# A GRU step on one core: three of the four blocks of R from h, Y with h stationary, the R seed ahead of Z

## The reference

```python
def step(H, xs):
    xz, xr, xh = xs            # X @ W.T + b, for all steps
    Z = sigmoid(xz + H @ Whz.T + bhz)
    R = sigmoid(xr + H @ Whr.T + bhr)
    H_tilda = tanh(xh + R * H @ Whh.T + bhh)
    H_new = Z * H + (1.0 - Z) * H_tilda
    Y = H_new @ Whq.T + bhq
    return (H_new, Y)
# result: x + Ys
```

## Time and profile before

| | |
|---|---|
| median of three runs | 581.74 us |
| the profiled execution | 582.49 us, of which the span is 580.4 us |
| PE busy | 556.9 us (96%), 49372 matmul records |
| PEld busy | 545.5 us (94%) |
| DVE busy | 322.7 us (56%) |
| ACT busy | 289.6 us (50%) |
| DMA | 16.2% of 16 engines on the queue of x and the output |
| granted clock of PE | full, but for one stretch near the start |

### The profile page before, as it was taken

The page is one execution under the profiler, slowest core; times in us unless marked ns, Lnnn a source line. Parts: engine busy times, 40 slices in busy tenths (PEclk is TensorE's granted clock), DMA queues, the critical chain, the costliest instruction groups (busy, mean ns, idle before and its releaser), DMA issues.

```text
span 580.4 us, 105994 instructions
## 1 busy us (share of the span) xinstructions
PE 556.9 (96%) x49372; PEld 545.5 (94%) x49372; DVE 322.7 (56%) x1802; ACT 289.6 (50%) x1671; POOL 0.2 (0%) x4
## 2 busy tenths in 40 slices
PE   7599999999999999999999999999999999999996
PEld 6589999999999999999999999999999999999996
DVE  1145555555555655555655555555555555555554
ACT  2145555545545555555455554554555555555553
POOL 0000000000000000000000000000000000000000
PEclk9599999999999999999999999999999999999999
DMA  4011111111111111111111111111111111111111
GB/s 154 17 35 48 41 50 45 41 52 43 45 50 41 49 46 42 52 42 45 50 41 49 45 41 50 45 45 50 41 46 49 41 50 45 45 50 41 47 48 46
DMA packets 57880, 27.58 MB, mean 48 GB/s; under 512 B 7056, under 2 KB 56976, under 8 KB 57872
## 3 DMA queue, kind: packets, MB, share of 16 engines
q1 hardware_dynamic: 56736, 26.63, 16.2%
q10 hardware_dynamic: 1136, 0.83, 0.4%
HBM read 18.91 MB, written 8.52 MB: 47 GB/s over the span
## 4 chain that ended last, share of the span: by engine, by line
PE 96%; issue 3%; DMA 0%; DVE 0%; ACT 0%; SPq 0%; DVEq 0%; ACTq 0%
PE r_ps L232 38%; PE c_ps L232 25%; PE z_ps L232 22%; PE y_ps L232 11%; DMA xres_sb<-in_xt_dram 0%; DVE o_sb L199 0%; SPq L122 0%; ACT c_ps L147 0%; DVE u_sb L218 0%; ACT r_ps L147 0%; ACT c_sb L174 0%; ACT z_ps L147 0%; DVEq L30 0%; DVE ones_sb L185 0%; DVE h_sb L223 0%
## 5 line engine op out<-in xcount | busy, mean ns | idle before, releaser
L232 PE MATMUL c_ps<-xt_sb,wx_sb 128*32 128x64 f32 x4128 | 174.6, 226 | 1.5 <-issue 1.5
L167 ACT ACTIVATE r_sb<-r_ps 128x32 f32<-128x32 f32 x512 | 74.3, 197 | 152.4 <-PE r_ps L232 152.4
L213 DVE TENSOR_TENSOR rh_sb<-r_sb,h_sb 128x32 f32<-128x32 f32 x512 | 75.1, 188 | 101.0 <-ACT r_sb L167 101.0
L232 PE MATMUL r_ps<-u_sb,whr_sb 128*32 128x32 f32 x8192 | 122.0, 198 | 8.9 <-issue 2.6
L232 PE MATMUL r_ps<-zh_sb,whr_sb 128*32 128x32 f32 x8192 | 124.9, 197 | 3.5 <-issue 3.5
L232 PE MATMUL z_ps<-h_sb,whz_sb 128*32 128x32 f32 x8192 | 124.5, 198 | 0.0
L218 DVE SCALAR_TENSOR_TENSOR u_sb<-z_sb,c_sb 128x32 f32<-128x32 f32 x512 | 75.2, 188 | 83.7 <-ACT c_sb L174 83.7
L232 PE MATMUL c_ps<-rh_sb,whh_sb 128*32 128x32 f32 x8192 | 121.7, 198 | 0.0
L232 PEld LDWEIGHTS r_ps<-u_sb,whr_sb 128*32 128x32 f32 x8192 | 103.4, 112 | 19.0 <-issue 19.0
L232 PE MATMUL y_ps<-h_sb,whq_sb 128*32 128x64 f32 x4128 | 118.2, 224 | 0.3 <-DVE o_sb L199 0.3
L232 PE MATMUL z_ps<-xt_sb,wx_sb 128*32 128x64 f32 x4128 | 113.7, 220 | 2.7 <-issue 2.7
(11 more groups left out here) (26 smaller groups left out, 257.5 us busy)
## 6 DMA issues: line engine op xcount, KB each, us to landing
xt_sb<-in_xt_dram SPq DMA_DIRECT2D x130, 64.0 KB, 1.8
xres_sb<-in_xt_dram SPq DMA_DIRECT2D x130, 64.0 KB, 1.8
out_dram<-o_sb SPq DMA_DIRECT2D x130, 64.0 KB, 1.6
wx_sb<-in_wx_dram SPq DMA_DIRECT2D x2, 256.0 KB, 4.3
wx_sb<-in_wx_dram ACTq DMA_DIRECT2D x1, 256.0 KB, 4.9
whz_sb<-in_whz_dram SPq DMA_DIRECT2D x1, 256.0 KB, 5.3
whr_sb<-in_whr_dram ACTq DMA_DIRECT2D x1, 256.0 KB, 6.0
whq_sb<-in_whq_dram SPq DMA_DIRECT2D x1, 256.0 KB, 6.3
```

Of the source, the lines that this page charges most:

```text
L167: nc.scalar.activation(r_sb[:, o], r_ps[:, o, here], ACT.Sigmoid).then_inc(s_r[o], 1)
L213: nc.vector.tensor_tensor(rh_sb[:, k], r_sb[:, k], old[:, k], ALU.mult).then_inc(s_rh[k], 1)
L232: return nc.tensor.matmul(ps, weights, moving, start=start, stop=False, skip_group_check=True, **kw)
```

## The change

R: of the four blocks of the product, one (k = 1, o = 0) stays split into a zh part, ahead of time, and a u part. The three others are taken from h itself, which was not needed there before. For this, h is added in two halves with a semaphore each (`s_h[k]`), and `rh_sb` waits for its half of h. The prologue does one block in place of four.

Y: a 32-column tile of h of one step is the stationary operand and 128 rows of `whq_sb` are moving, so Y comes out with the batch on the partitions. The four column tiles hold the two steps of a chunk and the two output halves, so one block does one half k of the contraction for all of the chunk: one block of four matmuls with 128 columns in a step, in place of two blocks with 64. The bias of Y, now a 128x128 tile, is written into PSUM by ACT once a chunk (`seed_y`), behind the sigmoid of Z in the second step; the first one ahead of the loop waits for the load of `bq_sb`. DVE adds the residual once a chunk, in its first step, in one instruction over 128 columns, with the residual's x and the output laid out to match.

Order: on ACT the R seed stands ahead of the sigmoid of Z. On PE the second x block of Z stands behind the candidate's blocks.

```diff
+            def seed_y(p):
+                return nc.scalar.copy(y_ps[p][:, 0, 0:P], bq_sb[:])
...
+            act.wait_ge(s_bq, DMA)
+            seed_y(1).then_inc(s_seed_y, CS)
...
+                    if s == 0:
+                        seed(r_ps[:, :, W * (1 - p):W * (1 - p) + W], R).then_inc(s_seed_r, CS)
                     act.wait_ge(s_z_ps, t + 1)
                     nc.scalar.activation(z_sb[:], z_view(p)[:, :, B * s:B * s + B], ACT.Sigmoid).then_inc(s_z, 1)
-                    if s == 0:
-                        seed(r_ps[:, :, W * (1 - p):W * (1 - p) + W], R).then_inc(s_seed_r, CS)
+                    if s == CS - 1:
+                        act.wait_ge(s_res, t + CS)
+                        seed_y(p).then_inc(s_seed_y, CS)
...
+            def residual(p, chunk, row_dmas):
+                dve.wait_ge(s_rows[p], row_dmas)
+                dve.wait_ge(s_y_ps, chunk + PAD + 1)
+                nc.vector.tensor_tensor(o_sb[:, p], y_ps[p][:, 0, 0:P], xres_sb[:, p], ALU.add).then_inc(s_res, CS)
...
-                    dve.wait_ge(s_h, t + 1)
                     for k in range(K):
+                        dve.wait_ge(s_h[k], t + 1)
                         dve.wait_ge(s_r[k], t + 1)
...
                     for k in range(K):
                         dve.wait_ge(s_u[k], t + 2)
-                    nc.vector.tensor_tensor(new, zh_sb[:], u_sb[:], ALU.add).then_inc(s_h, 1)
-                    residual(p, s, i * 2 + p - PAD, i * (2 * DMA) + DMA)
+                        nc.vector.tensor_tensor(new[:, k], zh_sb[:, k], u_sb[:, k], ALU.add).then_inc(s_h[k], 1)
+                    if s == 0:
+                        residual(p, i * 2 + p - PAD, i * (2 * DMA) + DMA)
...
-                return columns(y_ps[p][:, 0], slice(W * o, W * o + W), whq_sb, k, o,
-                               h_sb[:, k, CS * p:CS * p + CS], start=piece == 0)
+                for j in range(NQ):
+                    half, step = divmod(j, CS)
+                    last = mm(y_ps[p][B * j:B * j + B, 0, 0:P], h_sb[:, k, CS * p + step], whq_sb[:, k, P * half:P * half + P],
+                              tile_position=(0, B * j))
...
-                    for k in range(K):
-                        pe.wait_ge(s_u[k], t + 1)
-                        for o in range(K):
-                            r_mm = r_part(u, k, o, u_sb[:, k])
-                            if k == K - 1:
-                                r_mm.then_inc(s_r_ps[o], 1)
+                    pe.wait_ge(s_u[1], t + 1)
+                    r_part(u, 1, 0, u_sb[:, 1])
+                    pe.wait_ge(s_h[0], t + 1)
+                    r_part(u, 0, 0, old[:, 0]).then_inc(s_r_ps[0], 1)
+                    r_part(u, 0, 1, old[:, 0])
+                    pe.wait_ge(s_h[1], t + 1)
+                    r_part(u, 1, 1, old[:, 1]).then_inc(s_r_ps[1], 1)
...
-                    for piece in pieces:
-                        x_piece(q, Z, piece)
+                    x_piece(q, Z, pieces[0])
...
+                    x_piece(q, Z, pieces[1])
                     if s == 0:
                         pe.wait_ge(s_seed_r, t + 1)
...
                     pe.wait_ge(s_zh, t + 1)
-                    for k in range(K):
-                        for o in range(K):
-                            r_part((u + 1) % SLOTS, k, o, zh_sb[:, k])
-                    if s == 0:
-                        pe.wait_ge(s_res, t + 1)
-                    for piece in pieces:
-                        y_mm = y_piece(q, piece)
+                    for k, o in AHEAD:
+                        r_part((u + 1) % SLOTS, k, o, zh_sb[:, k])
+                    if s == 0:
+                        pe.wait_ge(s_seed_y, t + 1)
+                    y_mm = y_piece(q, s)
```

More of the change, by code:

```diff
@@ L20, with gru_kernel @@
 WARM = 60
-def gru_kernel(nc, xt, h0t, wx, whz, whr, whh, whq, bx, bh, bq, out):
+AHEAD = ((1, 0),)
+def gru_kernel(nc, xt, xr, h0t, wx, whz, whr, whh, whq, bx, bh, bq, out):
     fp32 = mybir.dt.float32
@@ L47, in gru_kernel @@
         b_sb = sb("b_sb", [P, K, 3])
-        bq_sb = sb("bq_sb", [P, K])
+        bq_sb = sb("bq_sb", [P, P])
         ones_sb = sb("ones_sb", [P, P], bf16)
         act_warm = sb("act_warm", [1, 1])
-        bq_seen = sb("bq_seen", [1, 1])
+        res_seen = sb("res_seen", [1, 1])
         xt_sb = sb("xt_sb", [P, 2, K, W])
-        xres_sb = sb("xres_sb", [P, 2, K, W])
-        o_sb = sb("o_sb", [P, 2, K, W])
+        xres_sb = sb("xres_sb", [P, 2, P])
+        o_sb = sb("o_sb", [P, 2, P])
         h_sb = sb("h_sb", [P, K, SLOTS, B])
@@ L97, in gru_kernel @@
         s_u = [sem(f"s_u{k}") for k in range(K)]
-        s_h = sem("s_h")
+        s_h = [sem(f"s_h{k}") for k in range(K)]
         s_zh = sem("s_zh")
@@ L190, in _ @@
                 nc.vector.memset(u_sb[:, k], 0.0).then_inc(s_u[k], 1)
[L191 to L202, removed]
+                nc.vector.memset(h_sb[:, k, CS], 0.0).then_inc(s_h[k], 1)
+            nc.vector.memset(res_seen[:], 0.0).then_inc(s_res, CS)
+            def residual(p, chunk, row_dmas):
+                dve.wait_ge(s_rows[p], row_dmas)
+                dve.wait_ge(s_y_ps, chunk + PAD + 1)
+                nc.vector.tensor_tensor(o_sb[:, p], y_ps[p][:, 0, 0:P], xres_sb[:, p], ALU.add).then_inc(s_res, CS)
             with dve.Fori(0, NIT) as i:
@@ L222, in _ @@
                         dve.wait_ge(s_u[k], t + 2)
[L223 to L224 removed]
+                        nc.vector.tensor_tensor(new[:, k], zh_sb[:, k], u_sb[:, k], ALU.add).then_inc(s_h[k], 1)
+                    if s == 0:
+                        residual(p, i * 2 + p - PAD, i * (2 * DMA) + DMA)
             for p in range(2):
[L226 to L227 removed]
+                residual(p, NC + p - PAD, NIT * (2 * DMA) + DMA)
         @block.tensor
@@ L247, in x_piece, with y_piece @@
                 return columns(ps, cols, wx_sb[:, gate], k, o, xt_sb[:, p, k])
-            def y_piece(p, piece):
-                o, k = divmod(piece, K)
-                return columns(y_ps[p][:, 0], slice(W * o, W * o + W), whq_sb, k, o,
-                               h_sb[:, k, CS * p:CS * p + CS], start=piece == 0)
+            def y_piece(p, k):
+                for j in range(NQ):
+                    half, step = divmod(j, CS)
+                    last = mm(y_ps[p][B * j:B * j + B, 0, 0:P], h_sb[:, k, CS * p + step], whq_sb[:, k, P * half:P * half + P],
+                              tile_position=(0, B * j))
+                return last
             def r_part(u, k, o, moving):
@@ L274, in _ @@
             pe.wait_ge(s_init, DMA)
-            for k in range(K):
-                for o in range(K):
-                    r_part(0, k, o, h_sb[:, k, SLOTS - 1])
+            for k, o in AHEAD:
+                r_part(0, k, o, h_sb[:, k, SLOTS - 1])
             pe.wait_ge(s_whz, DMA)
@@ L326, in _ @@
                     pe.wait_ge(s_zh, t + 1)
-                    for k in range(K):
-                        for o in range(K):
-                            r_part((u + 1) % SLOTS, k, o, zh_sb[:, k])
+                    for k, o in AHEAD:
+                        r_part((u + 1) % SLOTS, k, o, zh_sb[:, k])
                     if s == 0:
-                        pe.wait_ge(s_res, t + 1)
-                    for piece in pieces:
-                        y_mm = y_piece(q, piece)
+                        pe.wait_ge(s_seed_y, t + 1)
+                    y_mm = y_piece(q, s)
                     if s == CS - 1:
                         y_mm.then_inc(s_y_ps, 1)
[L337 to L340, removed]
+            pe.wait_ge(s_seed_y, T + 1)
+            for k in range(K):
+                pe.wait_ge(s_h[k], T + 1)
+            for k in range(K):
+                y_mm = y_piece(1, k)
             y_mm.then_inc(s_y_ps, 1)
@@ L361 @@
     chunks = x.transpose(2, 1, 0).reshape(K, P, NC, W).transpose(2, 1, 0, 3)
+    rows = x.reshape(B, NC, CS, K, P).transpose(1, 3, 2, 0, 4).reshape(NC, P, P)
     arrays = {
         "xt": np.pad(chunks, ((PAD, PAD), (0, 0), (0, 0), (0, 0))),
+        "xr": np.pad(rows, ((PAD, 0), (0, 0), (0, 0))),
         "h0t": np.asarray(cond_1024).T.reshape(K, P, B).transpose(1, 0, 2),
@@ L380 @@
                                    kind="ExternalInput").ap())
-    args.append(nc.dram_tensor("out_dram", (NC + PAD, P, K, W), mybir.dt.float32, kind="ExternalOutput").ap())
+    args.append(nc.dram_tensor("out_dram", (NC + PAD, P, P), mybir.dt.float32, kind="ExternalOutput").ap())
     gru_kernel(nc, *args)
@@ L384 @@
     rows = r.results[0]["out_dram"][PAD:]
-    return rows.reshape(NC, P, K, CS, B).transpose(4, 0, 3, 2, 1).reshape(B, T, C)
+    return rows.reshape(NC, K, CS, B, P).transpose(3, 0, 2, 1, 4).reshape(B, T, C)
```

9 lines of the change are left out of this document (4 added, 5 removed).

## The result

The changed kernel takes 557.83 us in the median of four runs (557.34 to 559.16); the kernel before takes 581.50. The ratio is 0.960, with a 95% interval of 0.957 to 0.963: 4% faster. The forecast was 562.0 us with 549 to 582 as its range.

A forecast was written before the change was run, and what follows sets the result against it. The prediction took PE as the old bound and the chain through h as the new one: 29.1 + 63 x 8.38 (528) + 3.1 = 560.2 us span, plus 2.1 around it, 562.3, given as 562.0 us; range 549 to 582.

The forecast's parts named there:

- the rival in which PE stays the bound: Rival: halves overlap better than the links say, so PE still bounds the step; 7.65 us a pass, 516 us; chance 0.05.
- The chain: Seven links from one step's first tanh through u, h, R's sigmoid, rh_sb and candidate to the next: 2.05 us.
- the path through the second halves: Same links by the second halves, each starting one to two blocks behind the first: same sum within 0.01 us.
- The disputed link, u to h: First half of h on DVE after u: 0.22 us taken; rival with second wait counting 0.29, 575.5 us, chance 0.20.
- the rival of the short group: Rival: sigmoid comes 0.46 us after R's first h block, not 0.33; step 2.18, 595 us; chance 0.07.
- The sign to look for: On PE, ahead of R from h: idle by some 0.2 us, released by DVE's h_sb.
- The loop turn: PE's 0.33 us at the end of a pass, beside the wait after Y, delays h's first block: 0.18 us a pass.
- The first pass: PE's code loading: five stalls instead of six, 3.8 us apart, so the second pass starts at 29.1 us.
- The end: After the last Y starts: 0.7 us for blocks and tail, 0.35 for DVE, 2.06 to the span's end; 3.1 us.
- Y: Y's one 128-column block on PE, in place of two with 64: 0.22 or, rounded, 0.23 us, against 0.24.
- The covers: Moved seeds and the wider residual cost nothing behind other work; the Y seed has 0.12 us to spare before the tanh.
- a failed cover: Rival: the cover of Y's seed or Z's sigmoid fails, taking back 0.07 to 0.1 us a step; 582 us; chance 0.06.

The follow-up runs named there:

- the experiment that forced the other case: Changed kernel with one more, always met, wait ahead of the first half of h, so u's wait stands in front: 582.87 us, ratio 1.002.

## Why the prediction was right, step by step

The bound changed hands as forecast: PE's records fell by some 128 a pass (769 to 642 in the windows), the clock stayed, and the chain by h set the step. That is shown from both sides: 0.07 off one link takes 18 us off the time, 0.09 more on another adds 25, and 0.22 more work on PE in each step costs 7. With a step of 2.08 against PE's 1.83, a pass of 8.32 and not 7.65, the rival in which PE stays the bound is out too. Against the terms of the sum:

- *The chain.* 2.05 predicted, 2.08 measured. Six of seven links are within 0.01 of their value; the seventh, candidate to tanh, was taken from the row of before as 0.47 and is 0.49, because R's two halves are now complete two blocks apart on PE: the second sigmoid, and with it the second half of `rh_sb`, comes 0.16 after the first instead of 0.10 (0.35 for both where the earlier trace rows has 0.29), and the candidate's second half waits for it on PE. The prediction had the sigmoids 0.13 apart (1.03 and 1.16), and held the path through the second halves to be the same within 0.01. The disputed link, u to h, is 0.23 against the 0.22 taken and 0.29 at the other end, and the experiment that forced the other case made it 0.32. The group of 8 records reached the sigmoid in 0.34 (0.33 taken), so the rival of the short group is out.
- *Where PE waits.* The sign to look for was some 0.2 ahead of R from h, released by `h_sb`. The larger wait, 0.15, lies ahead of R from u, and the table puts it down to `u_sb`; only 0.05 lie ahead of R from h. The sum of the chain does not change by that.
- *The loop turn.* 0.18 a pass predicted, 0.00 measured; this was the wrong term. I added its 0.33 to the end of Y (0.48 + 0.33 = 0.81). In the trace R from u starts 0.62 after the tanh at the turn and 0.58 elsewhere, ahead of h's 0.70. The turn is not a fixed length behind the last block: from Y's start to the next R it took 0.57 in the kernel before (0.24 of it work), 0.51 with Y in its old form, 0.53 with all of R split, 0.41 in the changed kernel. With as many records of Y, it is shorter where PE had waited more within the pass (16 records: 0.57 and 0.51; 8 records: 0.53 and 0.41). Why is open: that PE's sequencer runs ahead during such waits would fit, but no run tests it. With 0.03 more a step (0.12) and 0.18 less at the turn, a pass is 8.32 instead of 8.38: 3.8 us in 63 passes. That the pass came out so close is luck in part: the chain alone is 7.6 us too short in 63 passes, the turn 11.3 too long, and they cancel.
- *The first pass.* Five stalls in place of six, as said, 3.5 us apart (11.64 to 25.76), and the second pass starts at 26.9 instead of 29.1. One of these 2.2 us is there before the loop starts: it begins at 9.5 instead of 10.6, released by the load of `whh_sb`. That isn't the change's doing: the kernel before with only the seed moved also began at 9.5. The rest is hardly the clock's: that kernel had 1.00 through its first pass and took 22.0 us from the loop's start to the second pass; the kernel before, at 0.50 from 20 to 28 us, took 22.3; the changed one, at 0.75 from 20 to 24, took 17.4. The wait for `bq_sb` made ACT 0.3 us late once, under the first stall, as said.
- *The end.* 3.1 predicted, 3.9 measured, from the last Y (551.63) to 555.5. DVE's last instruction is released by PE, as said, but 1.20 after the block's start; 0.7 had been taken. Where the other 0.5 lies, no row shows. From DVE's end to the span's end there are 2.38 us where 2.06 had been taken.

```profile
551.63 0.65 PE L239 MATMUL y_ps<-whq_sb,h_sb 128*32 128x128 f32 x16 [0.27 <-DVE h_sb L230]
...
552.83 0.29 DVE L209 TENSOR_TENSOR o_sb<-y_ps,xres_sb 128x128 f32<-128x128 f32 x1 [0.97 <-PE y_ps L239]
```

- *Y.* 0.23 taken, 0.22 measured. The rule of the Trainium skill (TensorE: Matmul & The Clock Gate, Back-to-back issue gap), that starts are never closer than about 25 ns, does not hold for these matmuls, four side by side in column tiles: 24 records of R from h start within 0.22 us, 9 ns each.
- *The covers* held: Y's seed ran from 304.76 to 305.03 and the tanh started at 305.15 on its own time, 0.12 later as forecast. The residual over 128 columns takes 0.29 where I had 0.35. The clock stayed at 1.00 in steady passes, so the second failure mode of the clock that the Trainium skill tells of (same page, A second HAM failure mode) did not appear; the waits of this kernel are 0.05 to 0.15 us, and 0.19 at the loop turn.
- *Slips in the sums* that changed nothing here: 0.1 us a step of a failed cover would be some 588 us and not 584; the lower end of the range, 549, is 13 us below the forecast and not the 8 that the chain's 0.03 a step give; and the terms add up to 562.3, not 562.0.

What the forecast had not seen is how little R's part is worth here. The steps of the experiments add up: the seed 10 us (571.6), then Y in its new form with h in halves and the residual once a chunk, with all of R still split and Z's blocks in their old order, 8 us more (563.6), then R from h together with the moved block the last 6 (557.8). Of these 6, the pass has 0.04 x 63 = 2.5 (8.36 to 8.32), and the rest is the first pass with its one stall less (the second pass starts at 26.9 instead of 31.5). The kernel with only the second x block put back splits them another way: R from h by itself took 563.6 to 561.9, which is within noise, with a pass of 8.38 that is no shorter than 8.36; the moved block then took 4 us. PE was freed of 0.21 us a step, and the detour by h took back all of it. In the prediction it reads as if R's blocks carried the gain; the number came out right because the chain was summed up independently of them, and because the misses on chain and turn cancel in part.

## What to carry to other kernels

Where PE's order covers a chain exactly, price each edit twice: by what it takes off PE, and by the sum of the chain's links as they will be, and take the larger. That is what the forecast did right. A block moved past a wait counts as much as a block removed: an x block of 0.12 us moved behind the candidate cost 30 us, gained 4 us and cost 11 us in three neighbours of this kernel. Before moving any work, look at the order of the waits in front of the instructions on the chain: here the one that is met last has to be carried by the instruction, which gave 18 us for two swapped lines, and only 6 us where PE was the bound.

## What the runs showed of the hardware that I had not expected

- On DVE a releaser that a separate wait in front of the instruction waits for costs 0.07 us more than one that the instruction carries (sigmoid to `rh_sb` 0.30 against 0.23), and 0.09 to 0.10 where the front wait asks for two semaphores (0.32 against 0.23).
- The time that the turn of PE's loop adds depends on the work around it: 0.33 us in the kernel before, 0.19 at most in the changed one, and 0.08 where Y was issued twice.
- An addition of 128 columns out of PSUM takes 0.29 us, and the instruction before, with two additions over 64 columns, took 0.28. So twice the columns with one addition fewer cost 0.01; the two were not tried apart.
